# The second feed-forward of a decoder: two items moved among the attention's last units, and one product in place of three partition sums

## The reference, cut to what matters

```python
x = x + L1_xattn(_layernorm(x), ctx, ...)      # int8 attention, 16 heads of 16, keys of all batches together
x = x + L1_ffn(_layernorm(x), lut, gate_idx, up_idx, down_idx)
x = x + L2_attn(_layernorm(x), ...)            # a gated recurrence with its own feed-forward
...
def L1_ffn(x, lut, gate_idx, up_idx, down_idx):          # hidden 688, weights looked up in a table of 16
    h = jax.nn.silu(x @ lut[gate_idx].T) * (x @ lut[up_idx].T)
    return h @ lut[down_idx].T
def bit_linear(x, w, b):                                  # three weights of 256 x 1024 in L2_ffn
    gamma_w = jnp.clip(jnp.mean(jnp.abs(w)), 1e-05, None)
    w_dq = jnp.clip(jnp.round(w / gamma_w), -1.0, 1.0) * gamma_w
    ...
```

## Time and profile before

| | |
|---|---|
| median of three runs | 1686.45 us |
| lowest, highest | 1685.79, 1690.58 us |
| the profiled execution | 1685.58 us, of which its span is 1684.3 us |
| mean granted clock of TensorE | 0.874 of full speed |
| TensorE, VectorE busy | 85% and 68% of the span |
| ScalarE, GpSimd busy | 47% and 45% |
| last 128 units of the attention | 613 to 831 us |
| second feed-forward | 832.57 to 906.4 us |

### The profile page before, as it was taken

How to read it: one execution, slowest core, us unless ns; L and a number is a source line. 1 busy time by engine, 2 the same in 40 slices (tenths; PEclk the granted TensorE clock), 3 DMA queues, 4 the chain that set the end, 5 groups by cost and what they waited for, 6 DMA issues and landing times. The chain is left out here.

```text
span 1684.3 us, 25417 instructions
## 1 busy us (share of the span) xinstructions
PE 1432.6 (85%) x8102; PEld 1027.9 (61%) x8102; DVE 1137.5 (68%) x2964; ACT 799.3 (47%) x2003; POOL 761.0 (45%) x1211
## 2 busy tenths in 40 slices
PE   7999988899999979999798697385777677889999
PEld 4667754688888832333486586244555455558888
DVE  6877776367776588898555646776887678863222
ACT  3444442144334468788514434475656567752110
POOL 3888871165656547666422212435555423320000
PEclk9999997899999975555599898698888889999999
DMA  7000003000000045555420000012222256210000
GB/s 273 20 8 8 1 1 119 0 14 7 7 1 1 1 83 97 94 92 89 128 104 1 0 1 1 31 80 51 42 47 39 39 131 133 51 26 1 7 7 13
DMA packets 168835, 77.84 MB, mean 46 GB/s; under 512 B 156928, under 2 KB 161408, under 8 KB 167552
## 3 DMA queue, kind: packets, MB, share of 16 engines
q1 hardware_dynamic: 168704, 76.23, 19.5%
HBM read 37.40 MB, written 1.05 MB: 23 GB/s over the span
## 5 line engine op out<-in xcount | busy, mean ns | idle before, releaser
L101 PE MATMUL banks<-normed_t,arena_a 128*128 128x256 f32 x1120 | 257.6, 385 | 1.9 <-PEq L3625 1.9
L465 POOL TENSOR_TENSOR lut_weights<-lut_weights,arena_b 128x536 f32<-128x536 f32 x128 | 181.6, 1419 | 123.6 <-DVE arena_b L455 114.4
L101 PEld LDWEIGHTS banks<-normed_t,arena_a 128*128 128x128 f32 x1120 | 215.5, 194 | 32.7 <-issue 2.7
L597 POOL TENSOR_SCALAR work<-work,small 128x256 f32<-128x256 f32 (+1 forms) x384 | 176.4, 479 | 66.0 <-DVE small L589 65.8
L101 PE MATMUL banks<-arena_a 64*128 64x512 bf16 (+1 forms) x384 | 161.7, 540 | 16.4 <-ACT arena_a L1742 8.4
L1742 ACT ACTIVATE arena_a<-banks,work 128x1024 uint8<-128x1024 f32 x128 | 154.1, 1205 | 42.8 <-DVE work L1682 36.4
L107 PE MATMUL banks<-identity,work 128*128 128x128 f32 x1000 | 144.3, 287 | 29.6 <-ACT work L542 11.2
L1680 DVE TENSOR_REDUCE work<-banks 128x1 f32<-128x1024 f32 x128 | 155.4, 1214 | 20.0 <-PE banks L101 19.9
L1778 POOL TENSOR_SCALAR arena_a<-arena_a 128x1024 bf16<-128x1024 uint8 x128 | 132.4, 1047 | 56.5 <-DMA arena_a<-arena_a 54.6
L577 ACT ACTIVATE work<-banks,small 128x256 f32<-128x256 f32 (+1 forms) x258 | 115.1, 453 | 82.7 <-DVE small L564 55.8
L107 PEld LDWEIGHTS banks<-identity,work 128*128 128x128 f32 x1000 | 120.8, 149 | 53.7 <-POOL work L597 28.1
(11 more groups left out here) (457 smaller groups left out, 3174.5 us busy)
## 6 DMA issues: line engine op xcount, KB each, us to landing
arena_a<-in_L3f_wg SPq DMA_DIRECT2D x8, 512.0 KB, 3.9
arena_b<-in_lut_idx SPq DMA_DIRECT2D x8, 268.0 KB, 3.3
arena_b<-in_L_wqn SPq DMA_DIRECT2D x4, 512.0 KB, 9.7
arena_b<-in_L_wo SPq DMA_DIRECT2D x4, 512.0 KB, 13.0
arena_a<-in_L_wq SPq DMA_DIRECT2D x1, 2048.0 KB, 7.6
arena_a<-in_L_wo SPq DMA_DIRECT2D x1, 2048.0 KB, 12.6
arena_a<-arena_a SPq DMA_TRANSPOSE x128, 2.5
arena_b<-in_L2f_gv SPq DMA_DIRECT2D x1, 2048.0 KB, 7.9
```

Of the source, the lines that this page charges most:

```text
L101: ins = t.matmul(out, lhs_t, rhs, start=start and i == 0, stop=stop and i == n - 1)
L465: g.tensor_tensor(o, o, lut_t[j % 2], ALU.add).then_inc(*summed.up(c * LUT + j))
L597: ins = g.tensor_scalar(e[:, c], e[:, c], A.rl[n % 2][:, 2 * hh + i:2 * hh + i + 1], 0.0, ALU.mult, ALU.add)
```

## The change

1. The stage `l1_ffn` has no place of its own any more. `l1_cross` calls it and runs its generators: on TensorE one item behind units 128 and 132 of its loop, on ScalarE behind 130 and 133, on VectorE behind 131 and 134, and all the rest at the end of its own generators. The meeting between the two stages is gone. Items 0, 1, 2 wait for the exponentials of units 125, 126, 127, whose banks they take; the pairs are therefore 4, 0, 2 in turn.
2. Batch 3's turn moves from behind item 0 to behind item 3 (with down product 0) on TensorE, its copy behind item 3 on ScalarE. Its normalisation on ScalarE stands behind the attention's last copy and ahead of item 2's silu.
3. SyncE waits for the last tile's residual before it issues the loads.
4. The ternary weights' loads have a semaphore each. VectorE first takes the three sums of magnitudes (steps 1 to 3), then waits for one product on TensorE that adds all three columns over the partitions; it stands behind item 5 and writes three free columns of bank 3. One scale and one reciprocal serve all three. The GpSimd all-reduces are gone.
5. The twelve steps are dealt out otherwise: 2, 2, 1, 2, 1, 1, 2, 1 behind items 3 to 10, and none behind item 11. So the sums of weights 0 and 1 stand behind item 3, the third sum and the first rounding of weight 0 behind item 4, and one conversion behind item 10.

```diff
@@ l1_cross, tensor
-            yield MEET
+                if n in (128, 132):
+                    yield from some(items_tensor, 1)
+            yield from some(items_tensor, ALL_ITEMS)
@@ l1_cross, vector
-            yield MEET
+                if n in (131, 134):
+                    yield from some(items_vector, 1)
+            yield from some(items_vector, ALL_ITEMS)
@@ l1_cross, scalar
-            yield MEET
+                if n in (130, 133):
+                    yield from some(items_scalar, 1)
+            yield from norm_scalar("l1f", big_a, None, [3], both=True)
+            yield from some(items_scalar, ALL_ITEMS)
@@ l1_cross, gpsimd and sync
-            yield MEET
+            yield from ffn_gpsimd()
...
-            yield MEET
+            sp.wait_ge(*(yield added, s, NT - 1))
+            yield from ffn_sync()
@@ ternary_vector
-        v.wait_ge(*(yield ternary_in, "all"))
-        for n, src in enumerate((W["wg8"][:, 0:2048], W["wg8"][:, 2048:4096], W["wo8"])):
...
+        for n, src in enumerate(sources):
+            v.wait_ge(*(yield ternary_in[n // 2], "all"))
+            v.tensor_reduce(gam_sums[:, n:n + 1], src, AX.X, ALU.add, apply_absolute_value=True).then_inc(*vs.up(TERNARY, "sums", n))
             yield None
-            v.wait_ge(*(yield gs, TERNARY, "mean", n))
...
+        v.wait_ge(*(yield ts, TERNARY, "sums"))
+        v.tensor_scalar(gam[:, 0::2], ternary_sums, 1.0 / (P * 2048), 1e-5, ALU.mult, ALU.max).then_inc(*vs.up(TERNARY, "means"))
+        v.wait_ge(*vs.now())
+        v.reciprocal(gam[:, 1::2], gam[:, 0::2]).then_inc(*vs.up())
...
-    def ternary_gpsimd(n):
-        g.wait_ge(*(yield vs, TERNARY, "sums", n))
-        g.partition_all_reduce(gam[:, 2 * n:2 * n + 1], gam[:, 2 * n:2 * n + 1], P, bass.bass_isa.ReduceOp.add).then_inc(*gs.up(TERNARY, "mean", n))
+    def ternary_tensor():
+        t.wait_ge(*(yield vs, TERNARY, "sums", 2))
+        t.matmul(ternary_sums, ones, gam_sums, start=True, stop=True).then_inc(*ts.up(TERNARY, "sums"))
@@ l1_ffn
+        def pair(q):
+            return 2 * ((q + 2) % 3), [(gated_, s, q - 3)] if q >= 3 else [(exped, "l1x", H * NT - 3 + q)]
...
-                if q == 0:
+                if q == 3:
                     yield from norm_tensor(s, nf, high, [3], by_scalar=True)
+                if q == 5:
+                    yield from ternary_tensor()
...
-                    yield from some(back, 2 if q % 3 == 2 else 1)
+                    yield from some(back, (2, 2, 1, 2, 1, 1, 2, 1, 0, 0, 0)[q - 3])
```

More of the change, by code:

```diff
@@ L241, in build @@
     loaded = {n: signal(f"stage{n}_loads", 16) for n in (0, 1, 2, 3, 4, 6, 7, 8, 9, 10, 11)}
-    ternary_in = signal("ternary_weight_loads", 16)
+    ternary_in = [signal(f"ternary_weight_loads{i}", 16) for i in range(2)]
     stored = signal("store", 16)
@@ L321, in load_ternary @@
     def load_ternary():
[L322 to L324 removed]
+        sp.dma_start(W["wg8"], d["L2f_gv"]).then_inc(*ternary_in[0].up("all"))
+        sp.dma_start(W["wo8"], d["L2f_o"]).then_inc(*ternary_in[1].up("all"))
     ts, vs, as_, gs = signal("tensor_steps"), signal("vector_steps"), signal("scalar_steps"), signal("gpsimd_steps")
@@ L1911, in build @@
     TERNARY = "l2f"
-    gam = tiny[:, 100:106]
+    gam, gam_sums = tiny[:, 100:106], tiny[:, 124:127]
+    ternary_sums = banks[3].f[:, S:S + 3]
     def ternary_vector():
         tmp = work[:, 2048:4096]
-        v.wait_ge(*(yield ternary_in, "all"))
-        for n, src in enumerate((W["wg8"][:, 0:2048], W["wg8"][:, 2048:4096], W["wo8"])):
-            gm, dst = gam[:, 2 * n:2 * n + 2], W["tn8"][n]
-            v.tensor_reduce(gm[:, 0:1], src, AX.X, ALU.add, apply_absolute_value=True).then_inc(*vs.up(TERNARY, "sums", n))
+        sources = (W["wg8"][:, 0:2048], W["wg8"][:, 2048:4096], W["wo8"])
+        for n, src in enumerate(sources):
+            v.wait_ge(*(yield ternary_in[n // 2], "all"))
+            v.tensor_reduce(gam_sums[:, n:n + 1], src, AX.X, ALU.add, apply_absolute_value=True).then_inc(*vs.up(TERNARY, "sums", n))
             yield None
-            v.wait_ge(*(yield gs, TERNARY, "mean", n))
-            v.tensor_scalar(gm[:, 0:1], gm[:, 0:1], 1.0 / (P * 2048), 1e-5, ALU.mult, ALU.max).then_inc(*vs.up())
+        v.wait_ge(*(yield ts, TERNARY, "sums"))
+        v.tensor_scalar(gam[:, 0::2], ternary_sums, 1.0 / (P * 2048), 1e-5, ALU.mult, ALU.max).then_inc(*vs.up(TERNARY, "means"))
+        v.wait_ge(*vs.now())
+        v.reciprocal(gam[:, 1::2], gam[:, 0::2]).then_inc(*vs.up())
+        for n, src in enumerate(sources):
             v.wait_ge(*vs.now())
-            v.reciprocal(gm[:, 1:2], gm[:, 0:1]).then_inc(*vs.up())
-            v.wait_ge(*vs.now())
-            v.tensor_scalar(tmp, src, gm[:, 1:2], MAGIC, ALU.mult, ALU.add).then_inc(*vs.up())
+            v.tensor_scalar(tmp, src, gam[:, 2 * n + 1:2 * n + 2], MAGIC, ALU.mult, ALU.add).then_inc(*vs.up())
             yield None
@@ L2047, in later @@
                     yield from rec_turn_scalar("rec", q // 3 - 2)
-            yield from norm_scalar(s, nf, None, [3], both=True)
-            yield from turned_scalar(s, 3, high)
+                if q == 3:
+                    yield from turned_scalar(s, 3, high)
+                yield None
             yield from gated_scalar(F, later)
@@ L2056, in gpsimd @@
             for n in range(3):
-                yield from ternary_gpsimd(n)
                 yield from rec_gpsimd(n)
```

13 lines of the change are left out of this document (9 added, 4 removed).

## The result

The changed kernel took 1682.21 us (median of 16 runs, 1666.89 to 1693.1) beside 1686.93 for the kernel before (median of 16, 1679.06 to 1697.79) on the same chip. One of the 16 runs of the changed kernel, that of 1693.1, is a slow one and is left out of the ratio. The means of the others and of the runs before are 1680.2 and 1688.8 us; their ratio is 0.9949, with a 95% interval of 0.9927 to 0.9971. So the means lie 8.6 us apart and the medians 4.7, and 0.9949 of 1686.93 is 1678.3. The forecast was 1675.7 in a range of 1671.5 to 1681.8, with 10.8 us less. The change is faster, since the interval leaves out 1, by less than forecast; 1678.3 lies inside the range, the plain median of 1682.21 lies 0.4 us above it.

The account below looks back on a forecast made before the run. TensorE's own work bounds the stage, with gains at its ends: 7.1 us at the front, 5.3 after the ternary sums, 9.9 by the back, plus 0.9 clock: 10.8. From 1685.6 that gives 1674.8, plus 0.9 is 1675.7; range 1671.5 to 1681.8.

Parts of the forecast that it names:

- Item 0: Behind unit 128 on TensorE: takes 5.7 us, the clock rising 4 us after its start; bounds 5.36 and 7.7.
- From item 1 to item 3: Attention's end on TensorE: turns, copy and output product take 1.8 us instead of 3.2; item 3 starts 7.6 us earlier.
- the 0.5 of batch 3's turns: These turns stood before item 1 and now follow item 3, so 0.5 us comes off the 7.6 us gained.
- the front: Items 0 and 1 among the attention's units, without the meeting: a gain of 7.1 us.
- Rival (a): Clock falls once between items 1 and 2: 3 us lost, gain only 6.5 to 7.5, 1679.5 us; chance 0.27.
- The ternary loads: Issued about 834.6; first sum waits until 842.5, two sums end at 847.1, hidden with 3 us of cover before item 4.
- rival (b): Ternary loads land late because the next stage's share the queues: gain 5 us, 1681.4 us; chance 0.07.
- The product with ones: Behind item 5 on TensorE: 0.3 us plus 0.4 wait, then 0.8 wait before down product 1; gain shrinks to 5.3 us.
- The back: Wait before down product 3 is 2.0 us for 3.21, none before the last turn; total gain 9.9 us at next stage.
- The clock at the handover: Full clock in the next stage's first 16 records would pass on 1.8 us; the middle, 0.9, was taken.
- a 0.68 us turn wait: Second batch's recurrent turn no longer waits 0.68 us once the GpSimd all-reduces are gone: gain 5.3 becomes 5.9.
- A cover that was wrong: The next stage's largest load took 16.6 us and was said to be wanted 60 us later.

Follow-up runs that it names:

- one_allreduce: Changed kernel with one GpSimd all-reduce over three columns replacing the product with ones; next stage 81.8 us from unit 125's exponential (changed 78.3), ratio to kernel before 0.9922.
- no_meeting_items_late: Changed kernel with all items behind the attention, still without the meeting; next stage 83.7 us from unit 125's exponential (changed 78.3), ratio to kernel before 0.9950.
- last_conversion_earlier: Changed kernel with VectorE's last weight conversion behind item 9 instead of 10; next stage 77.2 us from unit 125's exponential (changed 78.3), ratio to kernel before 0.9910.
- third_item_early: Changed kernel with item 2 also behind unit 136 and the last conversion earlier; next stage 75.8 us from unit 125's exponential, ratio to kernel before 0.9933.
- allreduce_kept: Changed kernel without its ternary part: three GpSimd all-reduces and the old dealing stay; next stage 86.2 us from unit 125's exponential, ratio to kernel before 0.9969.
- front_undone: Changed kernel with items out of the unit loop and the meeting back; next stage 85.1 us from unit 125's exponential, ratio to kernel before 0.9960.
- allreduce_next_loads_later: Three all-reduces, one wait per ternary load, next stage's loads held until first ternary weights; next stage 92.8 us from unit 125's exponential, ratio to kernel before 1.0031.

## Why the prediction was right, point by point

- **Item 0**. It started 1.44 us behind E (predicted 1.37), but took 6.45 and 6.03 us in the two traces of this kernel and 6.09 to 6.58 in eight others, where the prediction took 5.7. The clock rose about 5.5 us behind its start, not 4, as two windows of the changed kernel show:

```profile
830.50:831.00 0.50, 0.50 (x2) 0.41 (x2) 0.00 (x0) 0.00 (x0) 0.45 (x1) 0.50 0.00 0
831.00:831.50 0.50, 0.50 (x3) 0.40 (x3) 0.00 (x0) 0.00 (x0) 0.50 (x1) 0.97 0.00 0
```

  This is the first mis-sized term, 0.3 to 0.8 us. Its bounds (5.36 and 7.7) held it.
- **From item 1 to item 3.** Turns, copy and output product took 1.87 us (1.8 predicted, 3.2 before). Item 3 starts 18.2 us from E (839.57 and twelve records, less 823.99), for 17.5 predicted and 25.2 before: 7.0 us sooner for 7.6. Less the 0.5 of batch 3's turns the front gives 6.5 for the predicted 7.1. Rival (a), a clock that falls between items 1 and 2, came in none of the ten traces that have the items early. The window of the changed kernel has TensorE busy 1.95 us of 3.5 at full clock:

```profile
836.10:839.60 3.50, 1.95 (x24) 1.50 (x23) 1.27 (x3) 0.37 (x1) 0.00 (x0) 1.00 0.00 0
```

- **The ternary loads**. VectorE waited for the first until 24.5 from E (23.3 predicted) and had 2.75 us to spare before item 4 (3 predicted): no rival (b).

```profile
848.47 4.48 DVE L1933 TENSOR_REDUCE tiny<-arena_b 128x1 f32<-128x2048 f32 x2 [1.90 <-DMA arena_b<-in_L2f_gv]
855.69 0.69 DVE L1900 TENSOR_TENSOR big_b<-big_b,banks 128x512 f32<-128x512 f32 x1 [2.75 <-PE banks L101]
856.30 2.28 DVE L1933 TENSOR_REDUCE tiny<-arena_b 128x1 f32<-128x2048 f32 x1
```

- **The product with ones**. Its two records took 252 and 273 ns (245 to 266 in the rows), 0.25 us together for 0.3; its wait was 0.46 for 0.4, and the one before down product 1 0.79 for 0.8. The gain there is 4.6 us in place of 5.3; what is missing is item 0's clock. The Trainium skill (GPSIMD Engine Reference, section "When to use GPSIMD"), by which a reduction over partitions is GpSimd's alone, is contradicted here, and one_allreduce gives the price of following it: 3.5 us in the distance, which the timed runs don't resolve.
- **The back**. 1.96 us before down product 3 (2.0 predicted, 3.21 before), none before the last turn (2.94 before), 1.82 to the next stage. Gain at down product 3 6.5 (7.1), at the next stage 9.4 (9.9 without the clock, 10.8 with it).
- **The clock at the handover**. The prediction took 0.9 between 0 and 1.8. The 16 records took 5.38 and 5.35 us for 5.75, so 0.4 was gained: the clock fell again, as the window of the changed kernel below shows. It stayed full in no_meeting_items_late, last_conversion_earlier and third_item_early, behind a wait of the same 1.82 us. This was the second mis-sized term, 0.5 us.

```profile
903.50:905.00 1.50, 1.50 (x5) 1.16 (x4) 0.10 (x1) 0.60 (x1) 1.25 (x5) 0.50 0.00 0
```

- **The step that was right only in company.** The prediction booked 7.1 us to the front as if it could stand alone, and a few tenths to GpSimd's all-reduces, a 0.68 us turn wait and the lateness at the end. The runs give 1.5 us for the front alone (87.7 to 86.2), 2.6 for the ternary part alone (to 85.1), and 9.4 for both: 5.3 of it belong to neither (0.7, 1.8 and 8.6 from the other trace of the kernel before, which leaves 6.1). Of the 5.3, 3.4 are the two falls of the clock in allreduce_kept (44 records 11.35 us for 9.66, 24 records 7.72 for 6.04), and the turn's wait of 3.61 us, which neither the kernel before nor front_undone has, is more than the rest. The first fall came behind the turn in all four kernels in which it waited 1.58 us or more; the second came in some traces and not in others behind waits of like size, so it may be chance. The sum came out because both parts were in it; a forecast of the front alone by the same working would have been wrong by more than 5 us. This is luck in part: the prediction nowhere says that the front needs the ternary part. The rows that would have told it were there: an all-reduce holds GpSimd 6.16 us before its record and 7.37 behind it, and in the kernel before these stood under TensorE's own work.
- **A cover that was wrong.** The next stage's loads are wanted by the first recurrent scaling, not 60 us later. The cover was 5 us, so the sum didn't suffer; allreduce_next_loads_later shows what it costs when it is gone.
- **The range.** Its lower end leaves out the 0.9 us that the forecast adds to the profiled execution: 11.7 and 2.5 below 1686.5 is 1672.3, not 1671.5. Its 2.5 us for later stages came from runs 4.8 apart; the 16 runs before the change lie 18.7 apart, so that the median of a few runs can fall inside this range or outside it by chance.

The two mis-sized terms account for 10.8 becoming 9.8 in the traces (9.4 and 0.4 at the handover). The rest of the difference to the 8.6 us between the means lies inside the ratio's interval (4.9 to 12.3 us), as does 10.8.

## What to carry to other kernels

A stage that starts earlier only helps if every chain beside it starts earlier too: before booking such a gain, list what the other engines' chains (here GpSimd's and the loads') have of cover against the new times, not the old. A sum over partitions of a few columns belongs on TensorE as a product with ones (0.25 us here) wherever a chain needs GpSimd next and the alternative holds it 13 to 22 us around a 0.4 us record. When a change is worth half a per cent of a long kernel, read the distance between two instructions around it within one trace, and leave totals to many timed runs.

## What the runs showed of the hardware that was not expected

- An all-reduce on GpSimd has a record of 0.40 us, with 5.8 to 6.2 us of nothing before it and 6.6 to 7.4 behind it. Beside loads at about 400 GB/s 10.8 and 12.0 us passed behind it, and 7.17 with the loads held back; before it 9.5 and 10.0, with the part of the loads not shown.
- TensorE's clock fell behind the one wait of 1.58 us at the recurrent turn (44 records 11.35 us for 9.66). Ahead of down product 3 it fell behind 1.96 us in two traces (24 records 7.72 and 7.68 us for 6.04) and stayed full behind the same wait in four; at the handover to the next stage it fell behind 1.8 us in six of nine (16 records 5.3 to 5.4 us for 3.69). A wait near 2 us costs itself or nearly twice that, and which of the two changes from trace to trace; the wait of 1.02 cost only itself in the three traces that have it.
- The GpSimd instruction on 128x2 elements behind the recurrent variance took 1.18 us beside VectorE's conversion of 2048 columns (allreduce_kept, L1964) and 0.19 beside its multiplication of an item (the changed kernel, L1965). The Trainium skill (GPSIMD Engine Reference, section "Specifications") has GpSimd share its SBUF interfaces with VectorE, with contention beside some of VectorE's instructions; these two rows agree, but don't show what about the instruction decides:

```profile
859.95 1.18 POOL L1964 TENSOR_TENSOR tiny<-tiny,mean_var 128x2 f32<-128x2 f32 x1
```

```profile
865.33 0.19 POOL L1965 TENSOR_TENSOR tiny<-tiny,mean_var 128x2 f32<-128x2 f32 x1
```
